# A deformable-convolution stage with half blocks, 32x32 matmul tiles and pixel stores begun by GpSimd

## What is computed

```
x = x + halo_attention(gn(x))
x = x + deform_conv(gn(x))
x = x + fourier(gn(x))
x = x + fft_conv(gn(x))
```

```
offset = conv3x3(x, offset_w) + offset_b          # 18 maps
mask   = sigmoid(conv3x3(x, mask_w) + mask_b)     # 9 maps
for each pixel (h, w) and tap k = (ky, kx):
    py, px = h - 1 + ky + dy[k], w - 1 + kx + dx[k]
    val[k] = bilinear sample of x at (py, px), zero outside
out = sum over k, c of dcn_w[o, c, k] * mask[k] * val[c, k]
```

## Time and profile before

| | us |
|---|---|
| median of 3 runs | 2114.85 |
| lowest, highest | 2094.2, 2151.25 |
| the profiled execution, its own time | 2127.27 |
| span of its records | 2125.5 |

### The profile page before, as it was taken

One profiled execution on the slowest core, in us unless ns is written; L12 is line 12 of the kernel. 1 busy time (PEld: TensorE's weight loads), 2 busy tenths in 40 slices (PEclk: granted clock), 3 DMA queues, 4 the chain that ended last, 5 costly groups with the idle time before them and its releaser, 6 DMA issues. The chain is left out here.

```text
span 2125.5 us, 58757 instructions
## 1 busy us (share of the span) xinstructions
PE 1895.2 (89%) x21269; PEld 1344.1 (63%) x21269; DVE 1278.3 (60%) x2688; ACT 1128.9 (53%) x3617; POOL 789.2 (37%) x743
## 2 busy tenths in 40 slices
PE   5599999999999998389999999596949999999998
PEld 3466666666666665145555556395827787778876
DVE  5178888888888888258878878642372222222222
ACT  2378888888888887357777778200211111111111
POOL 0077878878787876133323333000000011001100
PEclk9989999999999999589999999855879999999999
DMA  4400000000000000566666665240022111221110
GB/s 165 134 20 28 28 27 23 27 26 28 23 28 26 28 24 23 142 169 186 190 185 191 181 175 143 59 71 11 11 55 51 40 36 36 52 56 36 36 36 15
DMA packets 164173, 150.01 MB, mean 71 GB/s; under 512 B 60070, under 2 KB 151340, under 8 KB 163935
## 3 DMA queue, kind: packets, MB, share of 16 engines
q1 hardware_dynamic: 164014, 147.88, 26.2%
HBM read 83.18 MB, written 45.89 MB: 61 GB/s over the span
## 5 line engine op out<-in xcount | busy, mean ns | idle before, releaser
L412 ACT ACTIVATE at_probs<-at_sc,at_nmx 128x196 f32<-128x196 f32 x1152 | 473.0, 423 | 114.2 <-DVE at_nmx L358 114.2
L340 POOL TENSOR_TENSOR at_probs<-at_probs,at_rs 128x784 f32<-128x784 f32 x288 | 429.9, 1493 | 152.9 <-DVE at_rs L363 152.8
L358 DVE TENSOR_REDUCE at_nmx<-at_sc 128x4 f32<-128x784 f32 x288 | 277.4, 963 | 122.3 <-PE at_sc L436 122.3
L447 PE MATMUL at_pt<-at_ident,at_probs 128*98 128x128 f32 x2304 | 311.1, 278 | 40.6 <-DVE at_pts L368 40.0
L447 PEld LDWEIGHTS at_pt<-at_ident,at_probs 128*98 128x98 f32 x2304 | 241.1, 128 | 141.2 <-POOL at_probs L340 78.8
L436 PE MATMUL at_sc<-at_kw,at_qw 32*128 32x196 f32 x2304 | 272.1, 355 | 12.0 <-POOL at_qw L329 8.1
L1247 ACT ACTIVATE dn_mix<-dn_mps 128x432 f32<-128x432 f32 x384 | 182.3, 528 | 114.1 <-PE dn_mps L1142 110.6
L1930 POOL TENSOR_TENSOR fc_spo<-fc_prod 128x256 f32<-128x256 f32 x72 | 52.2, 725 | 502.6 <-DVE fc_prod L1974 502.6
L2031 PE MATMUL fc_qps<-fc_wk,fc_xs 99*128 99x128 f32 x1728 | 208.4, 278 | 31.3 <-DMA fc_xs<-in_ones 31.3
L412 ACT ACTIVATION_READ_ACCUMULATOR at_probs<-at_sc,at_nmx 128x1 f32 x1152 | 235.9, 205 | 0.0
L2031 PEld LDWEIGHTS fc_qps<-fc_wk,fc_xs 99*128 99x128 f32 x1728 | 202.0, 194 | 42.0 <-issue 39.1
(11 more groups left out here) (155 smaller groups left out, 2527.9 us busy)
## 6 DMA issues: line engine op xcount, KB each, us to landing
fc_xs<-fc_xp SPq DMA_DIRECT2D x144, 120.0 KB
dn_slab<-near_image SPq DMA_DIRECT2D x72, 200.0 KB, 4.2
at_vs<-attention_values SPq DMA_DIRECT2D x288, 49.0 KB
dn_offs<-near_maps SPq DMA_DIRECT2D x24, 486.0 KB
near_corners<-dn_split SPq DMA_DIRECT2D x24, 486.0 KB
dn_stack<-near_corners SPq DMA_DIRECT2D x24, 486.0 KB
dn_patch<-near_pixels SPq DMA_DIRECT2D x24, 384.0 KB
attention_values<-ap_vrow SPq DMA_DIRECT2D x21, 256.0 KB, 2.3
```

The source lines that it names most:

```text
L340: nc.gpsimd.tensor_tensor(probs[s][p][:, :, :, :], probs[s][p][:, :, :, :], rs[s][:, 2 * p:2 * p + 2, :].unsqueeze(3).broadcast_to([P, 2, ...
L358: nc.vector.tensor_reduce(nmx[s][:, 2 * p:2 * p + 2, :], sc[p][:, :, 0:2 * NK].rearrange("p b (j k) -> p b j k", j=2), AX.X, ALU.max, nega ...
L412: nc.scalar.activation(probs[s][p][:, b, j, :], sc[p][:, b, NK * j:NK * j + NK], ACT.Exp, bias=nmx[s][:, 2 * p + b, j:j + 1], accum_out=su ...
L447: mm = nc.tensor.transpose(pt[b % 2][0:HK, o:o + P], probs[s][p][:, b % 2, j, HK * c:HK * c + HK], ident[:, :])
```

## The change

Blocks are 8 columns wide and are treated as two halves of 4. A half needs 8 x 8 = 64 pixels, so one `mix` of 128 rows holds both halves and a step takes three blocks (`PER`): 4 steps per tile in place of 8, 96 in place of 192, each with the same 432 columns. `sample` uses 64 x 32 tiles, the halves on rows 0 to 63 and 64 to 127 and in two PSUM banks (`sps[0]`, `sps[1]`). `keep` runs twice per step. `stack` has 36 data partitions, in runs of 384 bytes, loaded by two DMAs; `offs` is loaded by three.

`conv` reads the normalised rows from an SBUF ring of 24 rows: 9 taps x 2 halves, each four 32 x 32 matmuls of 192 columns; `image` and `slab` are gone. `contract` has the same form. The two are interleaved, in k = 1 to 3, six (tap, half) each. `turn` and `conv` share the PSUM tile `cps`. `store_pixels` moves from SP to POOL. The preparation is one tile further ahead, and SP's order is new. Cut to its core:

```diff
-DBW = 12
-DSTEPS = W // DBW
+HBW = 4
+DBW = 2 * HBW
+NBLK = W // DBW
+PER = 3
+DSTEPS = NBLK // PER
+COLS = PER * TAPS * PX
-DATA = 18
+DATA = 36
@@ sync
             def load_maps(j):
                 sp.wait_ge(map_out, 16 * B * (j + 1))
                 if j >= 1:
-                    sp.wait_ge(corner_ready, 3 * j - 1)
+                    sp.wait_ge(hats_ready, HATS * j - 1)
+                    sp.wait_ge(corner_ready, 3 * j - 2)
+                for h, c, b, n in ((0, 0, 0, B), (1, 1, 0, B - 1), (1, 0, B - 1, 1)):
+                    sp.dma_start(offs[3 * TAPS * b:3 * TAPS * (b + n), h, :, :].rearrange("p a n -> p (a n)"),
             for t in range(DTILES):
                 if t + 1 < DTILES:
-                    store_corners(t + 1)
-                    load_patch(t + 1)
...
                     load_stack(t + 1)
...
                 if t + 3 < DTILES:
                     load_maps(t + 3)
+                if t + 1 < DTILES:
+                    load_patch(t + 1)
+                save(t)
+                if t + 4 < DTILES:
+                    store_maps(t + 4)
+                if t + 2 < DTILES:
+                    store_corners(t + 2)
@@ tensor
+                for at, row, rows in ((0, first, n), (n, 0, DR - n)):
+                    if rows > 0:
+                        for b in range(B):
+                            c, o = (b + h) % B, EDGE - 1 + kx + HBW * h
+                            out = cps[C * c:C * c + C, DPX // 2 * h + W // 2 * at:DPX // 2 * h + W // 2 * (at + rows)]
+                            part = ring[C * b:C * b + C, row:row + rows, o:o + W].rearrange("p r (k q) -> p r k q", q=DBW)[:, :, :, 0:HBW]
+                            mm = nc.tensor.matmul(out, wconv[C * b:C * b + C, tap, :], part, start=(i == 0), stop=(i == TAPS - 1))
+                for i in range(PER):
+                    for b in range(B):
+                        for h in range(2):
+                            c = (b + h) % B
+                            mm = nc.tensor.matmul(sps[h][C * c:C * c + C, n * i:n * i + n], patch[t % 2][side * h:side * h + side, PER * k + i, C * b:C * b + C],
+                                                  mix[s % 2][b][side * h:side * h + side, n * i:n * i + n], start=True, stop=True)
@@ the step loop of the tensor engine
+                    if k >= 1:
+                        for u in range(6 * k - 6, 6 * k):
+                            if t + 5 < DTILES:
+                                conv(t + 5, u)
+                            if t >= 1:
+                                contract(t - 1, u)
                     if t < DTILES:
                         sample(s)
+                    if k == 0 and t + 5 < DTILES:
+                        turn(t + 5)
@@ the step loop of the scalar engine
+                    if k == 0 and t + 4 < DTILES:
+                        bias_maps(t + 4)
                     if s + 1 < NSTEP:
                         for b in (2, 3):
                             relu(s + 1, b)
+                    if k == 0 and t + 2 < DTILES:
+                        prepare(t + 2, 3)
+                    if k >= 1 and t + 3 < DTILES:
+                        prepare(t + 3, k - 1)
+                    if k == 2 and t + 2 < DTILES:
                         high(t + 2)
@@ gpsimd
+            for g in range(2):
+                store_pixels(g)
             for j in range(DTILES):
                 scale(j)
                 corners(j)
                 rest(j)
+                if j + 2 < DTILES:
+                    store_pixels(j + 2)
```

More of the change, by code:

```diff
@@ L910, in _ @@
             sp.wait_ge(const_in, 16 * len(loads))
+        @block.gpsimd
+        def _(pool):
+            for tile in zeros:
+                nc.gpsimd.memset(tile, 0.0)
         @block.vector
@@ L987, in stage_deform_near, with stored @@
         sample_done, contracted, added = sem("sample_done"), sem("contracted"), sem("added")
+        conv_half, contract_half, border_out = sem("conv_half"), sem("contract_half"), sem("border_out")
         block = ctx.enter_context(nc.Block())
[L990 to L992 removed]
+        def stored(eng, g):
+            eng.wait_ge(pixels_out[g % 2], 16 * (DR + 1) * (g // 2 + 1))
         @block.sync
         def _(sp):
[L996 to L1022, removed]
             def load_patch(j):
                 for g in range(j, min(j + 2, DTILES)):
[L1026 removed]
+                    stored(sp, g)
+                if j == 0:
+                    sp.wait_ge(border_out, 32)
                 if j >= 2:
@@ L1173, in _ @@
             turn(1)
-            for kx in range(3):
-                conv(0, kx)
+            for u in range(2 * TAPS):
+                conv(0, u)
             turn(2)
-            for kx in range(3):
-                conv(1, kx)
+            for u in range(2 * TAPS):
+                conv(1, u)
             turn(3)
-            for kx in range(3):
-                conv(2, kx)
-            for kx in range(3):
-                conv(3, kx)
+            for j in (2, 3):
+                for u in range(2 * TAPS):
+                    conv(j, u)
+            turn(4)
+            for u in range(2 * TAPS):
+                conv(4, u)
             spread(0)
@@ L1261, in _ @@
             bias_maps(0)
+            prepare(0, 0)
             bias_maps(1)
-            for part in range(4):
+            for part in range(1, 4):
                 prepare(0, part)
+            bias_maps(2)
+            prepare(1, 0)
             high(0)
-            bias_maps(2)
-            for part in range(4):
+            for part in range(1, 4):
                 prepare(1, part)
+            bias_maps(3)
+            prepare(2, 0)
             high(1)
+            prepare(2, 1)
+            prepare(2, 2)
             for b in (2, 3):
@@ L1353, in _ @@
             keep_rows(1)
-            normalise(3)
-            normalise(4)
+            for g in range(3, 5):
+                normalise(g)
             keep_rows(2)
-            normalise(5)
             keep_rows(3)
-            largest(0)
-            largest(1)
-            largest(2)
+            for g in range(5, 7):
+                normalise(g)
+            for j in range(4):
+                largest(j)
+            keep_rows(4)
             for b in range(2):
```

351 lines of the change are left out of this document (170 added, 181 removed).

## The result

The changed kernel takes 2190.6 us (median of 4 runs, 2176.5 to 2205.8), the kernel before 2108.6 beside it (4 runs, 2094.2 to 2151.3): ratio 1.041, 95% interval 1.030 to 1.053. It is slower, as forecast (2183, range 2090 to 2295). Its profiled span is 2194.7 us. Times here are medians of all runs of a kernel, and ratios compare only runs within 1.5% of the fastest of the same kernel.

The account below looks back on a forecast made before the run. The preparation ring was taken to bound the kernel: 5.2 + 2.5 + 3.7 + 7.2 + 2.3 + 0.3 = 21.2 us per tile. The stage grows by 68, the profiled execution becomes 2195, the median 2183 us (range 2090 to 2295).

Parts of the forecast that it names:

- The ring: Once-per-tile loop of corners, stack, maps and preparation through SP, ACT and GpSimd: sets the tile at 21.2 us.
- D: Start of `distance_y(t+3)` on ACT in step 1; from there to the end of `high` 5.2 us.
- stack plus maps: Stack load to landing 7.2 us, then maps load 2.3 us on the same DMA engines.
- Where TensorE meets it: Sign: TensorE is idle in every tile, before the spread of the next tile.
- The other signs: ACT waits some 9 us per tile for maps, `distance_y` recurs every 21 us, DMA share about 0.5, relus halve.
- D(3): Start of `distance_y` for tile 3, after the lead-in: at 946 us, 18 us sooner if the clock rose early.
- D(23): Start of `distance_y` for tile 23, at 946 + 20 T; from there 59 us to the stage's end.
- T: Time per tile from one D to the next: 21.2 us, bounds 18.7 and 28.
- Rival 1: TensorE binds, not the ring: round trip under 6.5 us, tile 14.2 us, 2039 us; chance 0.14.
- Rival 2: Convolution's row tiles into one PSUM bank run one after another: T 31 to 55 us, 2510 or more; chance 0.05.
- Rival 3: A DMA start on GpSimd costs 2.5 us: T grows by 5.5 us, 2293 us; chance 0.09.
- Rival 4: The ring is there but quick, T from 17.5 to 19.5 us: about 2130 us; chance 0.12.

Follow-up runs that it names:

- maps first: Changed kernel with SP starting the next maps load ahead of the stack load, not behind it: 2146.1 us, ratio 1.014 to the kernel before.
- `high` early: Changed kernel with ACT doing `high` in step 1 ahead of `distance_y`, not in step 2 behind it: 2128.5 us, ratio 1.004.
- Without the patch: Changed kernel with patch loads of tiles 2 to 23 cut to three transfers of 16 short rows each: 2167.4 us, ratio 1.023.
- the split samples: Kernel before the change with each sample matmul cut into two halves of the same total columns: 2322.4 us, ratio 1.096.
- the wide kernel: Changed kernel with `high` a step earlier, convolution as nine taps of 384 columns, one transfer each for maps and stack: 2101.5 us, ratio 0.989.

## Why the prediction was right, step by step

- **The ring sets the tile**: right, and shown: ACT waits for the maps once a tile as said, and opening the ring at either end (maps first, `high` early) takes 2 to 3 us from the tile, and maps first takes that wait away. The parts of the ring, each waited for in all 20 turns, add up to the tile.
- **Its size**: 22.6 against 21.2. In the mean of 20 turns D to the end of `high` is 5.2 (5.2 said), `rest` 2.5 (2.5), corners 3.9 (3.7). The term that was too small is stack plus maps: 11.0 from the stack's start to distance_y against 7.2 + 2.3; together 22.6. Without the patch it is 8.9: the patch load on the same engines, which the sum priced at nothing, is what was missing.
- **Where TensorE meets it**: wrong in part. TensorE was to stand idle before the spread of the next tile; the longest wait by name is a convolution's for `pixrow`, 33.5 us against 13.1 before spreads. The other signs came: 8.8 us of wait for the maps a tile (9 said), DMA share 0.51 (0.5), half the relus (192 on VectorE, from 384).
- **The stops inside the ring**: TensorE's stops reach the ring only between D and `high`, where relus stand between ACT's parts. That stretch is 5.0 to 5.2 us in 17 of the 20 turns and some 4 us longer in all in the other three. So nearly all of the changed kernel's 42 us of "issue" lay in the ring's slack; they cost time only once the ring is open.
- **Lead-in and end**: D(3) was 937.9 against 946; the clock rose in the lead-in (0.86), where the sum kept it at half and gave 18 us for the other case; the end from D(23) took 64.5 us against 59.
- **The sum**: the stage grew by 94 us, 68 were forecast: 28 more by T, 8 less by D(3), 5.5 more by the end. That the profiled span came out at 2195 as forecast is the chance of the 24 us behind the stage; the ratio of the runs, some 87 us, is the better witness, and the forecast was about 20 short of it.
- **Rival 1** (TensorE binds, 14.2 us, 2039 us): the ring's part of its reasoning fell, and its price fell too. With the ring open the tile is 19.5 to 20.7 us in the mean, not 14.2. The tile of 14.2 counted TensorE's streams and not its instructions' way to it. Its own rows are 15.3 us at full clock, 1.1 more than said: 18 pairs of convolution and contraction take 7.4 us (0.41 each) in place of 5.9 and 0.6.
- **Rival 2** (row tiles into one bank run one by one): fell. The rows above have eight tiles within 0.45 us, and six contractions alone, one after another, would take 6 x 4 x 0.33 = 7.9 us where 2.15 were measured. The Trainium skill, TensorEngine Tiling (Array Packing), Gotcha 1, says that different row tiles can't access one bank at the same time; with each on its own 32 partitions the trace shows no such cost.
- **Rival 3** (GpSimd's start at 2.5 us): fell, 0.57 us.
- **Rival 4** (a quick ring, T from 17.5 to 19.5): fell, 22.6, and 20.1 even without the patch.
- **POOL's stores and the stack's two transfers** move the tile by 0.75 to 1 us each.

Left open: the two clocks behind the stage; and whether a queue of its own for the patch would remove both its wait and the stops.

## What to carry to other kernels

Before costing a rewrite by engine time, follow once the loop "load, prepare, store, load again" through the queues: here TensorE's and VectorE's parts were shorter and one line's place in ACT's order decided 60 us. And count instructions as traffic: the profile lists their packets among those of the 16 DMA engines that bring the data, and the split samples lost 8 us a tile beside 0.8 of work. So wide matmuls are worth more than their busy time says. Transfers begun apart took stops away here, but not time.

## What the runs showed of the hardware

- 16 KB of instructions are fetched for about 254 rows of TensorE. Up to 502 rows passed between two fetches in the wide kernel (389 at most in the kernel before). TensorE stopped for 1.5 to 6.5 us, and all 103 stops ended 2.2 to 3.8 us after a packet began; after a stop of 5.4 us the clock was 0.50.
- Doubling the sample matmuls at equal columns left the undisturbed step at 2.4 us and made the tile 9 us longer.
- Eight 32x32 tiles, four to a bank, ran side by side: 0.41 us for two groups of eight rows of 192 columns, 0.36 for the contraction's group alone.
- A GpSimd DMA start took 0.57 us.
